# Moving four projections ahead of and between the first maximum jobs, and GpSimd's addition of a bias behind the first normalisation, in a decoder kernel

## The reference

```python
x = x + mamba(layernorm(x))               # scan over 512 positions, 512 channels, 16 states
xn = layernorm(x)
q, k, v = heads(xn @ Wq + bq), heads(xn @ Wk + bk), heads(xn @ Wv + bv)     # 16 heads of 16
y  = softmax(causal(q k^T / 4)) v
qc, kc, vc = heads(xn @ Wcq + bcq), heads(ctx @ Wck + bck), heads(ctx @ Wcv + bcv)
y += softmax(qc kc^T / 4) vc
x = x + (y @ Wp + bp)
x = x + ffn(layernorm(x))                  # a dense part and 8 experts, 2 per position, mixed by a gate
```

## Time and profile before

| | |
|---|---|
| median of the runs | 1846.45 us (1843.0 to 1854.02) |
| profiled execution, its own time | 1853.68 us |
| its span | 1851.9 us |
| TensorE busy | 1474.7 us, 80% of the span |
| VectorE busy | 1306.0 us, 71% |
| ScalarE busy | 818.5 us, 44% |
| GpSimd busy | 660.6 us, 36% |
| mean granted clock of TensorE | 0.911 |

### The profile page before, as it was taken

One profiled execution on the slowest core, in us unless ns is written; L12 is line 12 of the kernel. 1 busy time (PEld: TensorE's weight loads), 2 busy tenths in 40 slices (PEclk: granted clock), 3 DMA queues, 4 the chain that ended last, 5 costly groups with the idle time before them and its releaser, 6 DMA issues. The chain is left out here.

```text
span 1851.9 us, 19445 instructions
## 1 busy us (share of the span) xinstructions
PE 1474.7 (80%) x6520; PEld 730.4 (39%) x6520; DVE 1306.0 (71%) x2025; ACT 818.5 (44%) x1586; POOL 660.6 (36%) x634
## 2 busy tenths in 40 slices
PE   5597889984987799875878899846677998779995
PEld 2353422242554232342544222422232322468884
DVE  6998488748996788379994887479976782533324
ACT  3543336745543266654433377443333566212221
POOL 2565341212864312117653422128643222112220
PEclk9799979996999899987999799969998899689998
DMA  4940452003002531021004520030014221147744
GB/s 132 340 134 1 111 126 56 23 3 127 18 1 54 142 77 34 13 92 53 1 0 119 118 56 25 1 118 21 0 43 128 64 48 63 53 147 253 230 160 137
DMA packets 128069, 153.87 MB, mean 83 GB/s; under 512 B 19110, under 2 KB 107695, under 8 KB 125921
## 3 DMA queue, kind: packets, MB, share of 16 engines
q1 hardware_dynamic: 124224, 143.96, 26.7%
q0 software_dynamic: 3744, 8.66, 1.3%
HBM read 102.82 MB, written 50.99 MB: 83 GB/s over the span
## 5 line engine op out<-in xcount | busy, mean ns | idle before, releaser
L170 PE MATMUL PS<-arena 128*32 128x512 f32 (+10 forms) x4150 | 830.2, 449 | 84.4 <-DVE maxs L1837 22.0
L170 PEld LDWEIGHTS PS<-arena 128*32 128x32 f32 (+3 forms) x4150 | 363.3, 128 | 524.4 <-ACT arena L1809 205.4
L1809 ACT ACTIVATE arena<-PS 128x512 f32<-128x512 f32 (+3 forms) x768 | 361.6, 549 | 225.5 <-PE PS L170 224.4
L1391 POOL TENSOR_TENSOR arena<-arena 128x1024 f32<-128x1024 f32 x128 | 305.0, 2384 | 238.7 <-DVE arena L1417 140.0
L1837 DVE TENSOR_REDUCE maxs<-PS 128x1 f32<-128x1024 f32 x256 | 297.8, 1214 | 41.5 <-PE PS L170 41.2
L1417 DVE TENSOR_TENSOR_SCAN arena<-PS,arena 128x1024 f32<-128x1024 f32 x128 | 292.1, 2282 | 6.1 <-ACT PS L1366 6.1
L1366 ACT ACTIVATE PS<-arena,A_neg 128x511 f32<-128x511 f32 x256 | 165.9, 681 | 240.8 <-DVE arena L1417 191.5
L170 PE MATMUL PS<-arena,ident 128*128 128x512 f32 (+1 forms) x560 | 259.6, 590 | 5.4 <-DVE arena L1426 5.4
L1426 DVE TENSOR_TENSOR arena<-arena,PS 128x1024 f32<-128x1024 f32 x128 | 156.3, 1221 | 6.9 <-PE PS L170 2.8
L1553 POOL TENSOR_SCALAR_AFFINE_SELECT arena<-arena 128x128 f32<-128x128 f32 x256 | 72.6, 294 | 234.2 <-ACT arena L1809 230.3
L170 PE MATMUL PS<-bc,bc_sel 96*128 96x512 bf16 x128 | 52.3, 409 | 121.3 <-DVE arena L1426 115.0
(11 more groups left out here) (263 smaller groups left out, 1548.1 us busy)
## 6 DMA issues: line engine op xcount, KB each, us to landing
arena<-in_ew SPq DMA_DIRECT2D x46, 512.0 KB
arena<-stack_parts SPq DMA_DIRECT2D x288, 64.0 KB, 2.3
rows_in<-nil SPq DMA_DIRECT2D x16, 1088.0 KB, 12.5
arena<-b_rows SPq DMA_DIRECT2D x16, 1024.0 KB, 8.0
stack_parts<-arena SPq DMA_DIRECT2D x40, 384.0 KB, 2.6
arena<-stack_parts SPq DMA_DIRECT2D x96, 128.0 KB, 4.2
arena<-rows_in SPq DMA_DIRECT2D x23, 272.0 KB, 4.7
xn<-dens SPq DMA_DIRECT2D x24, 256.0 KB
```

The lines of the kernel that those rows point to most:

```text
L170: return nc.tensor.matmul(o, l, r, start=start, stop=stop)
L1391: nc.gpsimd.tensor_tensor(b_sb[i % 2], u[:, 2 * kh:2 * kh + 2, :], Brow[:, n, :].unsqueeze(1).to_broadcast([P, 2, T]), ALU.mult).then_inc( ...
L1809: nc.scalar.activation(probs[(HG * s + h) % NPR][:, 0:N], ring_bank(n)[:, 0:N], ACT.Exp, scale=HD ** -0.5).then_inc(S["ring_read"], 1)
```

## The change

Two projections more (tiles 6 and 7) stand ahead of group 0's first maximum jobs; tiles 8 and 9 follow jobs 1 and 3. VectorE takes the residuals of tiles 6 and 7 ahead of the first reductions, those of 8 and 9 behind jobs 1 and 3, and none behind the first split. ScalarE's and GpSimd's order of tiles is the same. On SP's queue the load of the causal maxima stands ahead of the stores of tiles 8 and 9 (before: ahead of that of tile 9 alone). GpSimd's addition of `bp` moves from behind group 0's masks to behind group 0's normalisation, ahead of group 2's masks.

```diff
-            CK_TILES, FIRST_TILES = 2, 6
+            CK_TILES, FIRST_TILES = 2, 8
...
                 load_heads(0, 2)
-                for i in range(FIRST_TILES - 1, len(TILES)):
-                    if i == len(TILES) - 1:
-                        load_max_rows(0, CAUSAL)
+                for i in range(5, FIRST_TILES):
+                    store(i)
+                load_max_rows(0, CAUSAL)
+                for i in range(FIRST_TILES, len(TILES)):
                     store(i)
...
                 for k in range(TT):
                     masks(0, k)
-                if b == 0:
-                    pool.wait_ge(S["bp_ready"], 1)
-                link(nc.gpsimd.tensor_tensor(x1[:], x1[:], bp[:].unsqueeze(1).to_broadcast([P, TT, DM]), ALU.add))
                 pool.wait_ge(S["masked"], HG * TT)
...
                     nc.gpsimd.tensor_tensor(YT[g], y[0], y[1], ALU.add).then_inc(S["y_ready"], 1)
+                    if g == 0:
+                        if b == 0:
+                            pool.wait_ge(S["bp_ready"], 1)
+                        link(nc.gpsimd.tensor_tensor(x1[:], x1[:], bp[:].unsqueeze(1).to_broadcast([P, TT, DM]), ALU.add))
...
-                project(FIRST_TILES - 1)
+                for i in range(5, FIRST_TILES):
+                    project(i)
...
                 for i in range(KJOBS):
                     max_job(0, i)
-                    if i % 2:
+                    if i in (1, 3):
                         project(FIRST_TILES + i // 2)
...
-                for i in range(FIRST_TILES - 1, len(TILES)):
+                for i in range(5, len(TILES)):
                     high(i)
                     middle(i)
...
                 for i in range(KJOBS):
                     maxima(0, (i,))
-                    if i % 2 and i < KJOBS - 1:
+                    if i in (1, 3):
                         rest(FIRST_TILES + i // 2)
                 negated_parts(0, CAUSAL)
-                rest(len(TILES) - 1)
                 maxima(0, range(KJOBS, JOBS))
```

## The result

The changed kernel takes 1838.39 us, median of 20 runs (1835.35 to 1844.39); the kernel before took 1846.87 in 20 runs beside it (1843.0 to 1857.3). The ratio is 0.995, 95% interval 0.9938 to 0.9962: 8.5 us less, where 8.4 was forecast.

The account below looks back on a forecast made before the run. Bound by a chain of waits through each attention block's maximum jobs, transpose and split of maxima. 12.8 us gained less 4.4 lost gives 8.4: 1846.45 to 1838.0 us, range 1831 to 1846.

Parts of the forecast that it names:

- Tiles 6 and 7 ahead of the jobs: Two projections fill TensorE's idle time before the heads land: 12.8 us less in four blocks, bounds 9.6 and 14.6.
- L: Landing of the heads in each attention block, where the first maximum job starts; forecast not to move.
- T - L: Time from the heads' landing to the first transpose of the maxima (T); forecast 9.44 to 9.70 us per block.
- Tile 9's residual leaves the stretch behind T: Behind the first transpose VectorE loses a 0.75 us residual but waits for TensorE: 0, bounds 0 to 3.6 us gained.
- The rival that put a gain here: Behind the first transpose, 0.9 us gained per block if TensorE's clock is full; 1834.5 us, chance 0.12.
- GpSimd's addition: Behind the masks: memsets start earlier, so VectorE's cast waits for the second one's end, 1.1 us per block, 4.4 in all.
- a fixed slowdown: Other reading of the long cast: a memset beside it slows it by a fixed 1.3 us, making the addition's term 0.
- The new place of the addition: Behind group 0's normalisation, ahead of group 2's masks: hidden, taken as 0, bounds 0 to 0.5 us a block.
- L1858 beside a mask: VectorE instruction after group 2's cast: by the skill's rule 0.4 us late in all; prediction held the trace disagreed.
- The sum: Whole kernel: 12.8 less 4.4 gives 8.4 us saved, carried over whole to the median, 1838.0 us.
- TensorE delivers late: Rival between landing and first transpose: half-clock matmuls make VectorE wait, first term 8 or 9; 1842 us, chance 0.22.
- slower: Rival behind the split of the maxima: TensorE's half clock lasts twice as long, +19 us, 1865 us, chance 0.08.

Follow-up runs that it names:

- tiles alone: The changed kernel's tile order, with GpSimd's addition of bp back behind the masks; 1835.35 us, ratio 0.9918 to the kernel before.
- addition alone: The kernel before with only GpSimd's addition moved behind the first normalisation; 1857.81 us, ratio 1.0044.
- split from PSUM: The changed kernel with the maxima's middle part computed from PSUM instead of cast from SBUF; 1840.9 us, run again 1841.25 us.
- memset in eight: The changed kernel with each GpSimd memset of 3 x 4096 cut into eight of 3 x 512; 1835.91 us, ratio 0.9912.
- memsets late: The changed kernel with GpSimd's memsets of ones started only after VectorE has split the second maxima; 1836.29 us, ratio 0.995.
- filling: The changed kernel plus six matmuls per block, of unused results, around the first transpose of the maxima; 1848.01 us, ratio 1.0011.
- split from PSUM, filling: The changed kernel with both the middle part computed from PSUM and the six unused matmuls per block; 1837.41 us, ratio 0.9938.
- one tile fewer: The changed kernel with only tile 6 ahead of the maximum jobs, tiles 7, 8, 9 behind jobs 1, 3, 5; 1852.49 us, ratio 1.0033.
- tiles alone, split from PSUM: The changed kernel's tile order, addition back behind the masks, middle part of the maxima computed from PSUM; 1840.3 us, ratio 0.9949.
- the two delays: The kernel with the middle part from PSUM, TensorE starting each attention block 1.3 or 2.9 us later; 1843.94 and 1853.81 us.

## Why the prediction was right, point by point

The two terms, the waits behind them and their signs were right, and experiments show both. That 8.5 us came out for 8.4 is in part luck. The terms came to -14.4 and +4.5 for -12.8 and +4.4, a term put at 0 came to +1.4 and another to +0.5, and their sum stands in the blocks, 7.9 us. That the median followed the blocks was not shown by anything in the prediction, and in most of the kernels above it does not (us less than the kernel before; the blocks are those of one profiled execution each):

| kernel | in the blocks | in the median |
|---|---|---|
| changed | 7.9 | 8.5 |
| tiles alone | 13.9 | 13.1 |
| addition alone | -4.7 | -9.4 |
| split from PSUM, first and again | 18.6, 19.3 | 7.5, 4.3 |
| memset in eight | 17.7 | 12.5 |
| memsets late | 19.1 | 9.3 |
| filling | 5.2 | -2.5 |
| split from PSUM, filling | 17.3 | 8.1 |
| one tile fewer | 4.4 | -6.2 |
| tiles alone, split from PSUM | 17.0 | 8.0 |

- *Tiles 6 and 7 ahead of the jobs*: right, and 1.6 us larger than forecast, 14.4 for 12.8. VectorE's order and its cover were as worked out: first reduction at L + 1.30 (forecast 1.39), no wait of over 0.1 us behind it; tile 9 had no time to spare, its residual began at 1388.23, right behind ScalarE's copy. T - L came to 9.17 to 9.26 in place of 9.44 to 9.70. In the fourth block, of the 0.44 us, 0.09 are the earlier start, and VectorE's work took 7.91 us for the 8.26 of the sum: where a residual follows a reduction or the reverse, the two overlap by 0.08 to 0.09, and eight reductions in a row took 3.27 where the sum had twice 1.69. So the term lies near its upper bound of 14.6, but not for the reason that the bound gave. L itself was to stay; S to L differs by 1.5 us over four blocks, -1.35, -0.22, -1.64 and +1.68, which isn't one direction.
- *Tile 9's residual leaves the stretch behind T*: forecast 0, within 0 and -3.6. Measured +1.4, outside its bounds on the other side. TensorE's clock falls to half at T now, earlier against the first context job than before and for longer, so that job is ready only when VectorE would have been done with the residual anyway, and later. The two kernels with the filling show the clock's part, 0.7 us a block. The rival that put a gain here failed, and the reason given against it, that TensorE has little to do ahead of T, fits: with more work there the clock stayed full behind T in four of eight blocks.
- *GpSimd's addition*: forecast 4.4, measured 4.53 with the tiles and 4.2 without them. The reading of the earlier trace rows as a wait for the instruction's end was right and is shown by three runs; a fixed slowdown is ruled out by the 2.64 us.
- *The new place of the addition*: forecast 0 to 0.5 a block. The masks stayed covered. The cast of group 2 took 1.45, 1.03 and 0.47 us in the second to fourth block, each to 0.08 us behind the end of the addition, and held the reductions up by 0.28 in the second.
- *L1858 beside a mask* (L1861 in the changed kernel): here the prediction read its row wrongly. It took 0.28 us at 712.81, inside a mask that ended at 712.95, for a sign that this instruction, with two inputs in SBUF, doesn't wait for a GpSimd instruction that reads SBUF. But it ended at 713.09, 0.14 us behind the mask, which is just where it ends when it does wait: 0.14 behind the addition where it took 0.82 and 0.74 us, and 0.14 behind the mask where it took 0.39 (709.08 + 0.39 = 709.47, and 709.04 + 0.29 = 709.33). The row could not tell the two apart. The wait exists, and it is 0.11 us of the 0.28 above.
- *The sum*: 7.9 us in the blocks for 8.4. I took the saving to carry over whole because it is made of waits inside the span, and had not looked at what else moves. In this pair it did carry over, as with the tiles alone; in the other kernels 5 to 15 us were lost on the way. The range of 1831 to 1846 was not made for that.
- *TensorE delivers late* did not happen between L and T (the clock stayed full there); *slower* did not happen: behind the split the half clock lasted 13.7 us in each block, as before.

## What to carry to other kernels

Work that an engine can do while it waits for a transfer belongs ahead of the wait, all of it that fits: of two projections the first shortened the stretch from 51.3 to 43.7 us and the second to 36.9, 1.7 of it because TensorE kept its full clock in the second block. Before a copy from SBUF to SBUF on the critical path (or an operation with both inputs there, if GpSimd reads SBUF beside it), look at what GpSimd runs beside it and how long one instruction of that is; take one input from PSUM, or cut the GpSimd instruction. And cut two traces into the same pieces before comparing them: here 8 of 18 us lay in stages that the change does not touch. A saving in a stretch is shown by the stretch; what it is worth in the whole has to be measured over many executions, since here a gain of 17 to 19 us in the blocks left between 4 and 13.

## What the runs showed of the hardware

- A cast of 16 x 128 elements, 0.214 us by itself, took 1.50, 2.64, 0.57 and 0.28 us beside GpSimd: the first three as a copy from SBUF, each to within 0.1 us of the end of a GpSimd instruction, the last in another form with an input in PSUM.
- An operation with both inputs in SBUF (L1861) took its usual 0.28 us inside a GpSimd memset, in all four blocks of the split from PSUM. Beside GpSimd's addition, which reads SBUF, it took 0.82 and 0.74 us, and beside a mask 0.39, each time to some 0.14 us behind the end of the GpSimd instruction.
- The same stage of some 222 us, with the same instructions, takes 225 to 226 in other executions. What differs is where TensorE's clock falls to half (near 32 and 73.5 us behind the last transpose in the long ones); how long it is so in all need not differ (41.0 us in a stage of 226.06 and in one of 222.04). This comes and goes with the kernel and the execution. The Trainium skill ("TensorE: Matmul & The Clock Gate", section "Part 1: The HAM clock gate") says that the chip's watch on TensorE runs freely and does not start with the kernel, which would make such a thing possible; no run here shows that it is the cause, and the two delays that were to show it did not.
